# Layer norm behind the residual in the second and third attention layer: the row scaling goes from VectorE to ScalarE

## Chip, cores and metric

The kernel runs on one core of a Trainium2 chip. The metric is the time of one execution on the device, in microseconds (us), as the median of several runs. All the work here is float32 apart from a few small bf16 masks.

## The reference, cut to what matters

```
x = x + cross_attention_0(norm(x), ctx)            # layer 0
x = x + routed_attention_ffn(norm(x))              # the choice phase
h = norm(x)
h = _layernorm(h + self_attention(h), g1, b1)      # second layer of the attention code, "L1"
h = _layernorm(h + cross_attention(h, ctx), g2, b2)# third layer, "L2"
h = _layernorm(h + relu_ffn(h), g3, b3)            # late phase
x = x + h ;  x = x + moe_ffn(norm(x))              # late phase

def _layernorm(x, gamma, beta):
    mean = jnp.mean(x, axis=-1, keepdims=True)
    std = jnp.sqrt(jnp.mean((x - mean) ** 2, axis=-1, keepdims=True))
    return (x - mean) / (std + EPS) * gamma + beta
```

128 sequences of 64 tokens, width 128, 16 heads of depth 8. The change concerns `(x - mean) / (std + EPS)` of the layer norms with `g1, b1` and `g2, b2`. They stand behind the residual of L1 and L2.

## The kernel before

The 8192 tokens are cut into 16 groups of 512 tokens (8 sequences, 4 tiles of 128 rows). `attention_phase(..., (1, 2))` runs L1 and L2 as one pipeline of 32 steps. A step is one group's attention, and has eight slots `v` = 0 to 7, one for each unit of 8 heads on 128 tokens. In a step three groups are in work: the step's own group `g` (scores and softmax), the next group (its x, q, k and v are prepared: transposed, projected and copied, each in a slot of its own), and the group before (output projection, residual and layer norm, in two halves `m` = 0 and 1 of 256 tokens).

Each engine executes its own list in the order in which it is written, and the engines meet at semaphores. In slot `v`:

- TensorE (PE): in even slots the scores of units v and v+1 (L681, with a mask matmul at L668 or L675 ahead of it); the transposes of unit v-1 (L699), here T(v-1); the weighted sums of unit v-2 (L715), here W(v-2); then a preparation matmul if this slot has one (x transposes L642, q L648, k L646, v L651); in slots 0 and 4 the output's transpose (L724), in 1 and 5 the output projection (L733). T(7), W(6) and W(7) of a group run in slots 0 and 1 of the next step. Before each T(u) PE waits for VectorE's `shift(u)`.
- VectorE (DVE): `shift(v)` (the row maximum L491 and its subtraction L493), then the slot's other work: `divide`, `residual` of half 0 in slot 2 and of half 1 in slot 6, `normalise` of half 0 in slot 5 (L1) or 4 (L2), and `normalise` of half 1 at the end of slot 7, behind `shift(7)` and `divide`. The next instruction of DVE is then `shift(0)` of the next step.
- ScalarE (ACT): the exponential of unit v-1 (L398), then its preparation copies: in L1 the keys are spread in slots 5 and 6 (L365) and the values in slot 7 (L379); in L2 the keys in slots 0 and 1 and the values in slot 6.
- GpSimd (POOL): for each step the list is: inputs of the next group; `finish` of half 0; `with_bias` (L303, residual plus output bias, 128x512); `finish` of half 1. `finish` is a wait for the moments, the root `sd` (L309), a wait for `z_done`, then times gamma (L312) and plus beta (L315).

So the norm of one half goes DVE moments (L524), POOL root (L309), DVE `se`, `rs` and `z` (L531, L533, L536), POOL gamma and beta. In the last step of L2 there is no next group, so POOL's `with_bias` and all preparation are missing there.

Of the kernel before, what the change touches and what calls it, by code (L numbers as in the profile page):

```python
# [15 lines left out]
P = 128  # L16
# [96 lines left out]
def attention_phase(nc, ps, C, x_res, y_res, x_in, ctx_in, key_mask, run, ahead=(), setup=None):  # L113
# [11 lines left out]
    with ExitStack() as ctx:  # L125
        def sb(name, shape, dt=F32):
            return ctx.enter_context(nc.sbuf_tensor(f"{name}{a}", shape, dt))
# [34 lines left out]
        if post_norm:  # L162
            t1 = sb("t1", [P, 2, 2, D])
            st2 = sb("st2", [P, 2, 2, 6])
            mv2 = sb("mv2", [P, 2, 2, 2])
            sd2 = sb("sd2", [P, 2, 2])
            se2 = sb("se2", [P, 2, 2])
            rs2 = sb("rs2", [P, 2, 2])
            z2 = sb("z2", [P, 2, 2, D])
            zg2 = sb("zg2", [P, 2, 2, D])  # L170

# [38 lines left out]
        std2 = sem("std2")  # L210
        std2_eps = sem("std2_eps")
        rstd2 = sem("rstd2")
        z_done = sem("z_done")
        zg_done = sem("zg_done")
        y_done = sem("y_done")
# [60 lines left out]
        @block.gpsimd  # L276
        def _(pool):
            def rows_of(L, g):
                return tiles_of(x_res if L.a == 0 else y_res, L.own(g))

            def inputs_of(L, g, s, two_before):
                if L.pre_norm:
                    pool.wait_ge(var_eps, nth(g))
                    nc.gpsimd.tensor_tensor(rstd[:, :], veps[:, :], C["mhalf"][:, 0:TILES], ALU.pow
                                            ).then_inc(rstd_done, 1)
                    pool.wait_ge(rstd_done, nth(g))
                    nc.gpsimd.tensor_tensor(nmr[:, :], negmean[:, :], rstd[:, :], ALU.mult).then_inc(nmr_done, 1)
                else:
                    if two_before:

                        pool.wait_ge(prep_ready, nth(g - 2, NP, two_before.nr("xT")))
                        pool.sem_inc(passed, 1)
                    nc.gpsimd.tensor_copy(xn[:, s], rows_of(L, g)).then_inc(xn_ready, 1)

            def with_bias(L, g, s, first):
                if L.a == 1:
                    pool.wait_ge(xn_ready, nth(g))
                if not first:

                    pool.wait_ge(resid_done, g * 2 - 2)  # L300
                if L.a == 1 or not first:
                    pool.sem_inc(passed, 1)
                nc.gpsimd.tensor_tensor(xb[:, s], xn[:, s] if L.a == 1 else rows_of(L, g), across(L.bo, TILES), ALU.add  # L303
                                        ).then_inc(xb_ready, 1)

            def finish(L, g, m):
                if L.post_norm:
                    pool.wait_ge(moments2, nth(g, 2, m))
                    nc.gpsimd.tensor_tensor(sd2[:, m, :], mv2[:, m, :, 1], C["half"][:, 0:2], ALU.pow  # L309
                                            ).then_inc(std2, 1)  # L310
                    pool.wait_ge(z_done, nth(g, 2, m))
                    nc.gpsimd.tensor_tensor(zg2[:, m], z2[:, m], across(L.gam, 2), ALU.mult).then_inc(zg_done, 1)  # L312
                    pool.wait_ge(zg_done, nth(g, 2, m))
                    pool.sem_inc(passed, 1)
                    nc.gpsimd.tensor_tensor(tiles_of(y_res, L.own(g), 2 * m, 2), zg2[:, m], across(L.bet, 2), ALU.add  # L315
                                            ).then_inc(y_done, 1)

            def step(g, s, first, of, before, after):
                if after:
                    inputs_of(after, g + 1, 1 - s, before)  # L320
                if not first:

                    finish(before, g - 1, 0)
                if after:
                    with_bias(after, g + 1, 1 - s, first)
                if not first:

                    finish(before, g - 1, 1)
                if not after:
                    finish(of, g, 0)  # L330
                    finish(of, g, 1)

            def prep(g, s, L):
                if L.a == 0:
                    pool.wait_ge(consts_set, 1)
                    pool.wait_ge(pack_loaded, 16)
                inputs_of(L, g, s, None)
                with_bias(L, g, s, True)

            in_layers(pool, layers, prep, step)  # L340

        @block.scalar
        def _(act):
            def norm_apply(L, g, s, two_before):
                if not L.pre_norm:
                    return
                act.wait_ge(nmr_done, nth(g))
                if two_before:

                    act.wait_ge(prep_ready, nth(g - 2, NP, two_before.nr("xT")))  # L350
                    act.sem_inc(passed, 1)
                for t in range(TILES):
                    last = nc.scalar.activation(xn[:, s, t:t + 1, :], tiles_of(x_res, L.own(g), t, 1), ACT.Identity,
                                                bias=nmr[:, t:t + 1], scale=rstd[:, t:t + 1])
                last.then_inc(xn_ready, 1)
# [40 lines left out]
            def exps(g, u):  # L396
                act.wait_ge(t_ready, nth(g, UNITS, u))
                nc.scalar.activation(ex[:, u % 2], UB[u % 4].rearrange("p (c n) -> p c n", n=P), ACT.Exp  # L398
                                     ).then_inc(e_ready, 1)

            def copy_onT(L, g, m):

                act.wait_ge(onT_ready, nth(g, 2, m))
                nc.scalar.activation(onT[:, m], OB[m][:, 0:2 * P], ACT.Identity, bias=L.bv).then_inc(onT_copied, 1)
# [18 lines left out]
            def step(g, s, first, of, before, after):  # L423
                for v in range(UNITS):
                    if v > 0:
                        exps(g, v - 1)
                    elif not first:
                        exps(g - 1, UNITS - 1)
                    if v in (0, 4) and not first:
                        copy_onT(before, g - 1, v // 4)  # L430
                    if after:
                        prep_slot(after, g + 1, 1 - s, v)
                        if v == 2:
                            norm_apply(after, g + 1, 1 - s, before)
                if not after:
                    exps(g, UNITS - 1)
                    copy_onT(of, g, 0)
                    copy_onT(of, g, 1)

            act.wait_ge(vblk_set, 3)  # L440
            if a == 0:
                act.wait_ge(consts_set, 3)
            in_layers(act, layers, prep, step)

        @block.vector
        def _(dve):
# [60 lines left out]
            def residual(L, g, s, m):  # L507
                if m == 0:
                    dve.wait_ge(xb_ready, nth(g))
                dve.wait_ge(proj_ready, nth(g, 2, m))  # L510
                pr = PROJ[:, 256 * m:256 * m + 256].rearrange("p (t d) -> p t d", d=D)
                xs = xb[:, s, 2 * m:2 * m + 2, :]
                if not L.post_norm:
                    nc.vector.tensor_tensor(tiles_of(x_res, L.own(g), 2 * m, 2), pr, xs, ALU.add).then_inc(resid_done, 1)
                    return
                nc.vector.tensor_tensor(t1[:, m], pr, xs, ALU.add).then_inc(resid_done, 1)
                dve.wait_ge(resid_done, nth(g, 2, m))
                for t in (0, 1):
                    last = nc.vector.bn_stats(st2[:, m, t, :], t1[:, m, t, :])
                last.then_inc(stats2_done, 1)  # L520
                dve.wait_ge(stats2_done, nth(g, 2, m))
                dve.sem_inc(passed, 1)
                for t in (0, 1):
                    last = nc.vector.bn_aggr(mv2[:, m, t, :], st2[:, m, t, :])  # L524
                last.then_inc(moments2, 1)

            def normalise(L, g, m):
                if not L.post_norm:
                    return
                dve.wait_ge(std2, nth(g, 2, m))  # L530
                nc.vector.tensor_scalar(se2[:, m], sd2[:, m], EPS, None, ALU.add).then_inc(std2_eps, 1)  # L531
                dve.wait_ge(std2_eps, nth(g, 2, m))
                nc.vector.reciprocal(rs2[:, m], se2[:, m]).then_inc(rstd2, 1)  # L533
                dve.wait_ge(rstd2, nth(g, 2, m))
                for t in (0, 1):
                    last = nc.vector.tensor_scalar(z2[:, m, t, :], t1[:, m, t, :], mv2[:, m, t, 0:1],  # L536
                                                   rs2[:, m, t:t + 1], ALU.subtract, ALU.mult)
                last.then_inc(z_done, 1)

            def first_constants():  # L540
                nc.vector.memset(C["mhalf"][:, :], -0.5)
# [262 lines left out]
def nth(g, n=1, k=0):  # L804

    return g * n + (k + 1)
# [1418 lines left out]
```

## Time and profile before

| | us |
|---|---|
| median of 3 runs | 2162.67 (2158.76 to 2165.53) |
| the profiled execution | 2168.61 |
| its span in the trace | 2166.8 |
| L1 and L2 in the trace | about 642 to 1328 |
| one step of L1, in the middle | 21.6 |
| one step of L2, in the middle | 20.0 |

The times of the rows below are microseconds from the span's start. The profiled execution lies 6 us above the median of the runs. A step's length is the distance between the same instruction in two steps: `z` of half 1 starts at 822.91 and 844.53 in L1, and at 1275.38 and 1295.37 in L2.

### The profile page before, as it was taken

What the parts mean: (1) busy time and instruction counts of PE and PEld (TensorE: products, weight loads), DVE (VectorE), ACT (ScalarE), POOL (GpSimd) and SP (SyncE); (2) the same over time, 40 slices, a digit from 0 to 9 for tenths busy, and PEclk for the clock granted to TensorE, in tenths of its full rate; (3) what the DMA queues carried; (4) which work ended last, traced back from release to release, by engine and by line L of the source; (5) the groups of instructions that cost most, each with busy time, mean ns of one, the idle gap of its engine ahead of it and who ended that gap; (6) DMA issues with size and microseconds to landing.
All of it is one profiled execution on the core that took longest, in us unless ns stands there. A gap on an engine that the chain in (4) does not pass through costs nothing. (4 is left out here: it accounts for less than half of the span.)

```text
span 2166.8 us, 52756 instructions
## 1 busy us (share of the span) xinstructions
PE 1996.2 (92%) x19220; PEld 1546.9 (71%) x19220; DVE 1635.8 (75%) x4569; ACT 1065.2 (49%) x2180; POOL 465.8 (21%) x520
## 2 busy tenths in 40 slices
PE   7999994788869999999999998999999999999998
PEld 4666673666646666666666665767888888888887
DVE  5777776676536888888888884668888888888886
ACT  5656652556534555555545542543444444444442
POOL 1111110110101222222222222672211111112111
PEclk9999997999978999999999996999999999999999
DMA  3000000000000000000100002000000000000000
GB/s 126 30 29 27 21 10 1 1 1 0 1 20 2 0 0 0 0 0 21 30 29 19 29 10 66 1 1 1 11 6 5 6 10 5 6 5 10 5 5 10
DMA packets 27409, 30.50 MB, mean 14 GB/s; under 512 B 1952, under 2 KB 20640, under 8 KB 27040
## 3 DMA queue, kind: packets, MB, share of 16 engines
q1 hardware_dynamic: 27296, 29.18, 4.1%
q8 instruction: 48, 0.79, 0.1%
q14 instruction: 65, 0.53, 0.1%
HBM read 24.98 MB, written 4.19 MB: 13 GB/s over the span
## 5 line engine op out<-in xcount | busy, mean ns | idle before, releaser
L491 DVE TENSOR_REDUCE mx<-ps 128x8 f32<-128x512 f32 x384 | 262.3, 683 | 169.4 <-PE ps L681 169.3
L398 ACT ACTIVATE ex<-ps 128x512 f32<-128x512 f32 x384 | 230.2, 599 | 266.0 <-PE ps L699 263.8
L1125 ACT ACTIVATE y_res<-ps 128x512 f32<-128x512 f32 x288 | 172.4, 599 | 355.7 <-PE ps L1211 355.5
L1193 PEld LDWEIGHTS ps<-down,y_res 128*128 128x128 f32 x2048 | 267.2, 191 | 24.9 <-issue 3.0
L699 PE MATMUL ps<-pack,sh 128*128 128x128 f32 x1536 | 252.7, 287 | 27.6 <-DVE sh L493 26.8
L493 DVE TENSOR_TENSOR sh<-ps,mx 128x512 f32<-128x512 f32 x384 | 265.5, 691 | 13.2
L1193 PE MATMUL ps<-down,y_res 128*128 128x128 f32 x2048 | 270.5, 275 | 1.3 <-DVE y_res L1479 1.3
L715 PEld LDWEIGHTS ps<-vblk,ex 128*64 128x64 f32 x6144 | 214.7, 140 | 66.3 <-issue 66.3
L1461 DVE TENSOR_TENSOR y_res<-ps,y_res 128x512 f32<-128x512 f32 x288 | 197.9, 687 | 80.4 <-PE ps L1211 65.9
L715 PE MATMUL ps<-vblk,ex 128*64 128x32 f32 x6144 | 257.7, 227 | 0.0
L699 PEld LDWEIGHTS ps<-pack,sh 128*128 128x128 f32 x1536 | 170.3, 143 | 119.9 <-issue 63.7
L1479 DVE SCALAR_TENSOR_TENSOR y_res<-ps,late_comb,y_res 128x128 f32<-128x128 f32 x768 | 215.6, 344 | 23.8 <-PE ps L1193 11.6
L681 PE MATMUL ps<-kblk,qd 32*64 32x256 f32 x3072 | 208.3, 387 | 1.6 <-issue 1.5
L365 ACT ACTIVATE kblk<-ps,bkm,pack 128x512 f32<-128x512 f32 x192 | 139.0, 783 | 23.5 <-PE ps L646 23.5
L1209 PE MATMUL ps<-late_x_lo,late_gate_hi 128*128 128x512 f32 x288 | 136.7, 475 | 12.5 <-DVE y_res L1461 12.5
L681 PEld LDWEIGHTS ps<-kblk,qd 32*64 32x64 f32 x3072 | 108.8, 135 | 54.3 <-issue 9.9
L1031 POOL TENSOR_TENSOR y_res<-y_res 128x512 f32<-128x512 f32 x48 | 62.0, 1292 | 369.6 <-ACT y_res L1118 369.6
L1211 PE MATMUL ps<-late_x_hi,late_up_hi 128*128 128x512 f32 x288 | 114.2, 397 | 0.0
L1209 PE MATMUL ps<-late_x_lo,late_up_hi 128*128 128x512 f32 x288 | 113.6, 395 | 0.0
L1211 PE MATMUL ps<-late_x_hi,late_gate_hi 128*128 128x512 f32 x288 | 113.6, 394 | 0.0
L1210 PE MATMUL ps<-late_x_hi,late_gate_lo 128*128 128x512 f32 x288 | 112.5, 391 | 0.0
L1210 PE MATMUL ps<-late_x_hi,late_up_lo 128*128 128x512 f32 x288 | 111.8, 388 | 0.0
(237 smaller groups left out, 3419.8 us busy)
## 6 DMA issues: line engine op xcount, KB each, us to landing
ctxT<-in_ctx SPq DMA_DIRECT2D x32, 256.0 KB, 2.7
x_res<-in_x SPq DMA_DIRECT2D x16, 256.0 KB, 2.7
kmi<-in_key_mask SPq DMA_DIRECT2D x16, 256.0 KB, 3.2
out<-y_res SPq DMA_DIRECT2D x16, 256.0 KB, 2.3
pack<-in_pack SPq DMA_DIRECT2D x1, 2053.0 KB, 9.8
wqkv<-in_wqkv SPq DMA_DIRECT2D x1, 1536.0 KB, 10.9
gate<-in_gate SPq DMA_DIRECT2D x6, 192.0 KB, 3.7
up<-in_up SPq DMA_DIRECT2D x6, 192.0 KB, 3.7
```

The costliest lines, as they stand in the source:

```text
L398: nc.scalar.activation(ex[:, u % 2], UB[u % 4].rearrange("p (c n) -> p c n", n=P), ACT.Exp).then_inc(e_ready, 1)
L491: nc.vector.tensor_reduce(mx[:, u % 2], sc, AX.X, ALU.max).then_inc(max_done, 1)
L493: nc.vector.tensor_tensor(sh[:, u % 4].rearrange("p (h k) -> p h k", k=S), sc, mx[:, u % 2].unsqueeze(2).broadcast_to((P, HH, S)), ALU.sub ...
L681: last = nc.tensor.matmul(outs[w][64 * b:64 * b + 64, t * HQ * S:(t + 1) * HQ * S], qd[rows, s, n * S:(n + 1) * S], kblk[rows, s, n].rearr ...
L699: last = nc.tensor.transpose(UB[u % 4][:, c * P:(c + 1) * P], sh[:, u % 4, c * P:(c + 1) * P], ident)
L715: last = nc.tensor.matmul(OB[m][64 * b:64 * b + 64, col:col + 32], ex[:, u % 2, c, b * S:(b + 1) * S], vblk[:, s, 2 * (2 * m + t) + b, pai ...
L1193: last = nc.tensor.matmul(YB[k % 2][:, t * D:(t + 1) * D], act_[:, k % 3, t * P:(t + 1) * P], down[:, k, :], start=True, stop=True)
L1209: nc.tensor.matmul(out, hi, y, start=True, stop=False)
L1210: nc.tensor.matmul(out, lo, x, start=False, stop=False)
L1211: return nc.tensor.matmul(out, hi, x, start=False, stop=True)
L1461: V.tensor_tensor(act_[:, k % 3], UB[k % 2], sg[:, k % 2], ALU.mult).then_inc(act_ready, 1)
L1479: last = V.scalar_tensor_tensor(acc[:, s, t], y[:, t], comb[:, s, t, k - SH:k - SH + 1], acc[:, s, t], ALU.mult, ALU.add)
```

## The change

DVE no longer computes `z = (t - mean) * rs`. After `rs` it makes a bias for each row, `nm = -mean * rs` (128x2, one small instruction for both tiles of a half), and signals `nmr2_done`. ScalarE makes `z = t * rs + nm` with one ACTIVATE for each tile of 128 rows and signals `z_done`. It does so for half 0 at the end of its slot 6 and for half 1 at the end of its slot 7. `z_done` starts at 2, and DVE's `residual` waits until ScalarE has read the `t` of the group before, in the same buffer.

```
@@ pool: finish(L, g, m)
-                    pool.wait_ge(z_done, nth(g, 2, m))
+                    pool.wait_ge(z_done, nth(g, 2, m) + 2)
@@ scalar, new
+            def scale_rows(L, g, m):
+                if not L.post_norm:
+                    return
+                act.wait_ge(nmr2_done, nth(g, 2, m))
+                for t in (0, 1):
+                    last = nc.scalar.activation(z2[:, m, t:t + 1, :], t1[:, m, t:t + 1, :], ACT.Identity,
+                                                bias=nm2[:, m, t:t + 1], scale=rs2[:, m, t:t + 1])
+                last.then_inc(z_done, 1)
@@ scalar: step, at the end of slot v
+                    if v >= 6 and not first:
+                        scale_rows(before, g - 1, v - 6)
                 if not after:
...
+                    scale_rows(of, g, 0)
+                    scale_rows(of, g, 1)
@@ vector: residual
+                dve.wait_ge(z_done, nth(g, 2, m))
+                dve.sem_inc(passed, 1)
@@ vector: normalise
-                for t in (0, 1):
-                    last = nc.vector.tensor_scalar(z2[:, m, t, :], t1[:, m, t, :], mv2[:, m, t, 0:1],
-                                                   rs2[:, m, t:t + 1], ALU.subtract, ALU.mult)
-                last.then_inc(z_done, 1)
+                nc.vector.scalar_tensor_tensor(nm2[:, m], mv2[:, m, :, 0], -1.0, rs2[:, m], ALU.mult, ALU.mult
+                                               ).then_inc(nmr2_done, 1)
```

ScalarE's list at the end of a step of L2's loop, in the kernel before (`vblk` are the values of the next group, `ex` the exponentials of units 5, 6 and, in the next step, 7):

```order
L398 ACTIVATE ex<-ps 128x512
L376 REGISTER_ALU
L379 COPY vblk<-ps 64x4x8x8 x4
L397 REGISTER_ALU
L398 ACTIVATE ex<-ps 128x512
L397 REGISTER_ALU
L398 ACTIVATE ex<-ps 128x512
```

The same place in the changed kernel:

```order
L400 ACTIVATE ex<-ps 128x512
L378 REGISTER_ALU
L381 COPY vblk<-ps 64x4x8x8 x4
L408 ACTIVATE z<-t,nm,rs 128x128 x2
L399 REGISTER_ALU
L400 ACTIVATE ex<-ps 128x512
L408 ACTIVATE z<-t,nm,rs 128x128 x2
L399 REGISTER_ALU
L400 ACTIVATE ex<-ps 128x512
```

Half 0's `z` now stands behind the copy of the values, half 1's between the exponentials of units 6 and 7.

POOL's list for one step of L1's loop, which keeps its order, in the changed kernel:

```order
L310 ISA
L311 TENSOR_TENSOR sd<-mv,half 128x2
L313 REGISTER_ALU
L314 TENSOR_TENSOR zg<-z,pack 128x256
L317 ISA
L317 TENSOR_TENSOR y_res<-zg,pack 128x256
L302 ISA
L305 TENSOR_TENSOR xb<-xn,pack 128x512
L310 REGISTER_ALU
L311 TENSOR_TENSOR sd<-mv,half 128x2
```

The second `sd`, the root of half 1, stands behind half 0's gamma and beta and behind `xb`, before and after the change; what is new is the engine for whose `z` the first `zg` waits.

## Rows read from the trace of the kernel before

**Rows 1.** The page's slices of the span, 40 of 54.2 us each: granted TensorE clock in tenths.
```profile
PEclk9999997999978999999999996999999999999999
```

**Rows 2.** Windows: length, then busy us of PE, PEld, DVE, ACT, POOL; granted clock; DMA.
```profile
700.00:970.00 270.00, 258.23 (x3541) 176.95 (x3540) 222.84 (x607) 147.43 (x287) 78.96 (x111) 1.00 0.00 0
990.00:1298.00 308.00, 299.89 (x4124) 211.30 (x4118) 269.98 (x649) 157.75 (x293) 86.52 (x124) 1.00 0.08 24
1298.00:1328.00 30.00, 28.85 (x255) 20.41 (x254) 16.18 (x45) 6.20 (x11) 4.67 (x7) 0.51 0.00 1
642.00:664.00 22.00, 20.48 (x165) 12.07 (x164) 9.76 (x23) 6.49 (x14) 2.49 (x3) 0.51 0.00 1
```

**Rows 3.** Waits in L2, 990 to 1298 us: total, times, longest.
```profile
DVE mx L491 <- PE ps L681: 23.7, 31, 1.2
```

**Rows 4.** Groups by line, 640 to 1310 us: busy us, mean ns of one.
```profile
L536 DVE TENSOR_SCALAR z<-t,mv,rs 128x128 f32<-128x128 f32 x120 | 36.2, 344 | 2.2
L353 ACT ACTIVATE xn<-x_res,nmr,rstd 128x128 f32 (+1 forms) x60 | 24.6, 482 | 0.0
```

**Rows 5.** Timeline of L1, end of a step: start, duration, idle before.
```profile
840.60 1.44 ACT L365 ACTIVATE kblk<-ps,bkm,pack 128x512 f32<-128x512 f32 x2
...
841.45 1.28 POOL L303 TENSOR_TENSOR xb<-xn,pack 128x512 f32<-128x512 f32 x1 [1.47 <-DVE t L516]
...
842.69 0.71 POOL L309 TENSOR_TENSOR sd<-mv,half 128x2 f32<-128x2 f32 x1
...
844.14 0.16 DVE L531 TENSOR_SCALAR se<-sd 128x2 f32<-128x2 f32 x1
...
845.07 0.69 DVE L491 TENSOR_REDUCE mx<-ps 128x8 f32<-128x512 f32 x1
```

**Rows 6.** Timeline of L2, end of a step and start of the next.
```profile
1112.35 1.09 POOL L303 TENSOR_TENSOR xb<-y_res,pack 128x512 f32<-128x512 f32 x1 [3.14 <-DVE t L516]
...
1112.67 1.50 ACT L379 COPY vblk<-ps 64x256 f32<-64x256 f32 x4 [1.08 <-PE ps L651]
...
1113.40 0.71 POOL L309 TENSOR_TENSOR sd<-mv,half 128x2 f32<-128x2 f32 x1
...
1115.02 0.16 DVE L531 TENSOR_SCALAR se<-sd 128x2 f32<-128x2 f32 x1
...
1115.93 0.68 DVE L491 TENSOR_REDUCE mx<-ps 128x8 f32<-128x512 f32 x1
...
1116.10 0.64 POOL L312 TENSOR_TENSOR zg<-z,pack 128x256 f32<-128x256 f32 x1 [1.99 <-DVE z L536]
...
1117.02 0.64 POOL L315 TENSOR_TENSOR y_res<-zg,pack 128x256 f32 x1 [0.28 <-POOL zg L312]
...
1117.39 0.42 PEld L699 LDWEIGHTS ps<-pack,sh 128*128 128x128 f32 x4 [0.32 <-DVE sh L493]
```

**Rows 7.** Timeline of PE in L2: T(0), T(1) mid-loop, then in the last step.
```profile
1277.36 0.66 PE L699 MATMUL ps<-pack,sh 128*128 128x128 f32 x4
...
1280.38 0.66 PE L699 MATMUL ps<-pack,sh 128*128 128x128 f32 x4
...
1297.35 0.66 PE L699 MATMUL ps<-pack,sh 128*128 128x128 f32 x4 [0.99 <-DVE sh L493]
...
1301.86 1.11 PE L699 MATMUL ps<-pack,sh 128*128 128x128 f32 x4
```

**Rows 8.** A window of the choice phase: PE busy, then granted clock.
```profile
421.00:422.00 1.00, 0.00 (x0) 0.71 0.00 0
```

**Rows 9.** Timeline of PE in L1, T(1) and W(3): first step, then a later one.
```profile
650.34 1.11 PE L699 MATMUL ps<-pack,sh 128*128 128x128 f32 x4
...
663.08 0.95 PE L715 MATMUL ps<-vblk,ex 128*64 128x32 f32 x16
...
828.13 0.66 PE L699 MATMUL ps<-pack,sh 128*128 128x128 f32 x4
...
835.91 0.66 PE L715 MATMUL ps<-vblk,ex 128*64 128x32 f32 x16
```

More of the change, by code:

```diff
@@ L168, in attention_phase @@
             rs2 = sb("rs2", [P, 2, 2])
+            nm2 = sb("nm2", [P, 2, 2])
             z2 = sb("z2", [P, 2, 2, D])
@@ L212, in attention_phase @@
         rstd2 = sem("rstd2")
+        nmr2_done = sem("nmr2_done")
         z_done = sem("z_done")
@@ L442, in _ @@
                 act.wait_ge(consts_set, 3)
+            if post_norm:
+                act.sem_inc(z_done, 2)
             in_layers(act, layers, prep, step)
```

## The prediction

> **What bounds the kernel now.** I began with the slices of the span. L1 and L2 lie in slices 12 to 25, and the reader should see that the TensorE clock is granted in full there, but not in the slices at their two edges [rows 1]. The windows say the same in figures: in the middle of L1 PE is shown busy 258 us of 270, DVE 223 and ACT 147, in the middle of L2 300, 270 and 158 of 308 [rows 2]. DVE and PE bound these layers together. ACT is half idle, and to give it DVE's work looks free. The third view is the waits: DVE waits for scores about twice in a step (23.7 us in 31 waits over L2) [rows 3]. In those places a shorter DVE list buys nothing. The fourth is the timeline of a step's end, which decides here. PE stands before T(0) and waits 0.32 us for DVE's shift(0), which stands behind `normalise` of half 1 [rows 6]. So this `normalise` is on the path that sets the step's length, and whatever it waits for is too.
>
> **Half 0, taken from DVE.** `z` costs DVE 36.2 us over 60 halves, 0.60 us a half [rows 4]. For half 0 it stands in slot 5 (L1) or 4 (L2), and the next scores come late afterwards [rows 3]. I count nothing for its removal; the wait for scores grows by what is saved. `nm`, 128x2 on DVE, isn't in the trace. From below it costs 0 (then all 0.60 us are saved), from above 0.60, as much as the `z` that it replaces. The nearest row is `se`, also 128x2, with 0.16 us [rows 5]. I take 0.17, so a `normalise` gets 0.43 us shorter.
>
> **Half 0, put on ACT.** An ACTIVATE of 128x128 with scale and bias from a column is there already, 482 ns [rows 4], so two take 0.96 us. ACT has the time, but the place decides. In L1 the two stand behind the spread of the keys, which ends at 840.60 + 1.44 = 842.04 [rows 5]. In L2 they stand behind the copy of the values, which ends at 1112.67 + 1.50 = 1114.17 [rows 6]. Today half 0's `z` is long done by then. POOL waits for it, and behind POOL's wait stand, in this order, gamma, beta, `with_bias` and the root `sd` of half 1. DVE's `normalise` of half 1 waits for that root, and behind it stands shift(0). The chain is new:
>
> - L1: 842.04 + 0.96 (`z`) + 0.92 (start of gamma to start of beta [rows 6]) + 0.64 (beta [rows 6]) + 1.28 (`xb`) + 0.71 (`sd`) = 846.55. Today `se` starts at 844.14 [rows 5]. DVE comes 2.41 us later to it.
> - L2: 1114.17 + 0.96 + 0.92 + 0.64 + 1.09 + 0.71 = 1118.49, against 1115.02 [rows 6]: 3.47 us later.
>
> Hand-overs of about 0.1 us between engines are left out, and so is an overlap of the two ACTIVATEs; they roughly cancel. From each I take off the 0.43 us of the shorter `normalise`: shift(0), and T(0) behind it, come 2.0 us later in L1 and 3.0 in L2. All that PE can do ahead of T(0) it has then done, and nothing later in the step gives the time back, because each following pair of slots hangs on T(0) through scores and exponentials.
>
> How many steps: L1's loop has 14 (2.0 us each); the last step of L1, the first of L2 and L2's loop have L2's preparation slots, 16 steps (3.0 each). The last step of L2 has neither copy nor `with_bias`, so no stall, and the end of the layer costs under 1 us more. Sum: 28 + 48 = 76 us.
>
> **Half 1 on ACT.** It waits for `nm` and delays the exponential of unit 7. W(7), which needs that, stands behind T(0), and T(0) needs shift(0), 1.4 us of DVE work after `nm`; 0.96 us of `z` and the exponential fit within that and T(0) itself. Nothing, then; without that cover it would be up to 0.5 us a step. The exponential of unit 6 in L2 comes 0.96 us later, within the stall. The new wait of `residual` is for a `z` from the step before, done a slot or more earlier: nothing.
>
> **What the stall does to the clock.** PE's wait before T(0) grows from about 0.3 us to some 2.3 in L1 and 3.3 in L2. In the last step of L2 a wait of 0.99 us stands at the same place [rows 7], and from 1298 on the granted clock is at its lower level, 1.2 GHz, for the rest of that step (mean 0.51) [rows 2]. The only other difference there is that no key projection ran before the wait. In the choice phase the clock falls inside a stretch in which PE does nothing [rows 8]. I therefore expect a fall in each of the 30 stalled steps. How long does it stay down? In the first step of L1 it is down up to 664 (mean 0.51) and full later [rows 2]; 664 is just behind the q projection of slot 4, ahead of W(3) [rows 9]. So a visit lasts from T(0) to the q projection, if that suffices. Its price, from rows at both levels:
>
> - T(0) to T(1): 1301.86 - 1297.35 = 4.51 against 1280.38 - 1277.36 = 3.02 [rows 7], 1.5 us more.
> - T(1) to W(3), which follows q: 663.08 - 650.34 = 12.74 against 835.91 - 828.13 = 7.78 [rows 9], 5.0 us more.
>
> That is 6.5 us. A projection need not suffice: those of the prologue, ahead of 642, had not lifted the clock [rows 2]. Then it stays down to the next one, k in L1 a slot later or v in L2 two slots later, with the projection itself some 3 to 6 us of work (a slot is an eighth of a step, 2.5 to 2.7 us). At the ratio 12.74 / 7.78 = 1.64 that costs 2 to 4 us more. I give that 4 cases in 10 and take 8.0 us a visit (estimated from these rows). The price is bounded by 0 below (no fall) and 13 above (down for the whole step: 0.64 x 20.0 to 21.6). 30 x 8.0 = 240 us.
>
> **A rule of the skill.** The trace first: a wait of 0.99 us was enough for the fall [rows 7]. The Trainium skill, page "TensorE: Matmul & The Clock Gate", section "HAM oscillation", tells of a kernel whose clock falls in waits for a DMA of about 3 to 5 us, longer than L1's stall. By that the clock would fall in L2 at most: the second rival. The trace doesn't agree with it as a lower bound, at least where little matmul work surrounds the wait.
>
> **The sum.** 2168.6 + 76 + 240 = 2484.6 for the profiled execution. It lay 6 us above the median of the runs, so I predict 2479 us.
>
> **Rivals.**
>
> 1. *The clock holds.* Only the stall: 2163 + 76 = 2239 us. For it: mid-loop, L1 and L2 hold the full clock over short waits [rows 2]. Against: [rows 7], with a third of the stall.
> 2. *The clock falls in L2 alone*, where the stall is longest: 76 + 16 x 8 = 204, 2367 us. L1's stall is 2.0 us with the value projection and the mask matmuls close ahead, which speaks a little for it.
> 3. *The clock stays down through nearly all of both layers.* PE is then last itself and hides the stall: 30 x 13 = 390, 2553 us. For it: 22 us at a stretch at the start of L1 [rows 2]. Against: the loops bring three projections a step.
> 4. *Faster.* If POOL had half 1's root ready before DVE reached `se`, only the 0.43 us would count, and T(0) can move by 0.32 at most, since PE then bounds it: 30 x 0.3 = 9 us, 2154. It decides at ACT: half 0's `z` would have to end about 3.4 us before 1115.02, at 1111.6 in L2, ahead of the copy of the values, which starts only at 1112.67 [rows 6]. The list of ACT excludes that, unless the hardware did the POOL work much faster than its rows.
> 5. *Nothing measurable:* the late `z` takes some other slack that I don't see. Nothing in the profile speaks for it.
>
> **Chances.** Forecast 0.60, rival 1 0.12, rival 2 0.13, rival 3 0.08, rival 4 0.03, rival 5 0.04. A measurement of this kernel tells 0.3% (6.5 us) from no change. That gives slower 0.93, within 0.3% 0.04, faster 0.03. The likeliest case alone has 2430 to 2530 (6.5 to 9.5 us a visit). The range goes down to rival 1 and up just short of rival 3: 2235 to 2540.
>
> **What would show it.** In the changed profile: DVE's `se` of half 1 idle 2.4 us (L1) and 3.4 us (L2) with POOL's root as the one that ended the wait; POOL's gamma of half 0 released by ACT's `z`, at the end of ACT's keys or values; PE's T(0) waiting for `sh` for 2 to 3 us; steps of about 31 to 32 us where they were 21.6 and 20.0; granted clock around 0.7 to 0.8 in the slices of both layers, rising behind a projection; all other phases as long as before. I am wrong on the stall if `se` waits under 1 us; on the clock if the slices of both layers read 1.00; on the direction if T(0) doesn't wait longer than 0.3 us.

## Result and profile after

The changed kernel takes 2444.92 us (median of 6 runs, 2443.73 to 2448.55) against 2164.1 us before (6 runs): 1.1304 times as long, 95% interval 1.1279 to 1.1329, or 280.8 us more. It is slower, as forecast; the predicted time of 2479 us was 34 us too high. The executions of the kernel before differ among themselves: of the 23 measured beside the first four experiments, 12 have a mean granted clock of 0.970 or more and a median of 2160.8 us, 11 have 0.965 to 0.968 and 2168.9 us; the profiled one (0.967) is of the second kind.

The page after, the same rows of slices as [rows 1], now 61.1 us each. L1 and L2 lie in slices 11 to 27:

```profile
DVE  5777766765365555556555555547788888888886
ACT  5666625666344444444333333345444434444343
POOL 1111111110022222221111111137411111111211
PEclk9999979999687777778777777779999999999999
```

Every engine, ACT too, is now less busy there, and from slice 13 to 27 the granted clock reads 7 (once 8) instead of 9. The windows, as in [rows 2] (length, busy us of PE, PEld, DVE, ACT, POOL, clock). The middle of L1, then the middle of L2:

```profile
700.00:970.00 270.00, 248.78 (x2491) 164.52 (x2487) 149.94 (x406) 118.01 (x238) 53.07 (x76) 0.72 0.00 0
1150.00:1560.00 410.00, 368.22 (x3617) 246.98 (x3616) 234.04 (x543) 159.52 (x309) 73.61 (x107) 0.72 0.05 16
```

DVE was busy for 223 of the same 270 us of L1 before and is busy for 150 now: it gets through two thirds of the work in the same time. Outside the two layers nothing changed: in the choice phase (335 to 640 us) PE is busy 219.6 us before and 219.4 after. Layer 0 and the late phase, first before, then after:

```profile
0.00:335.00 335.00, 307.30 (x4036) 217.23 (x4036) 231.98 (x530) 196.04 (x385) 39.87 (x52) 1.00 0.12 39
1340.00:2166.00 826.00, 802.05 (x4921) 690.65 (x4919) 654.69 (x2096) 360.20 (x727) 202.68 (x171) 1.00 0.03 9
```

```profile
0.00:335.00 335.00, 307.77 (x4036) 217.66 (x4036) 231.80 (x530) 195.81 (x385) 39.88 (x52) 1.00 0.12 39
1617.00:2442.00 825.00, 800.89 (x4921) 689.13 (x4919) 654.16 (x2096) 359.86 (x727) 202.67 (x171) 1.00 0.03 9
```

The same late work that began at 1340 begins at 1617; the loss is between. The waits from 700 to 1500 us (total, times, longest) name it:

```profile
POOL zg L314 <- ACT z L408: 463.9, 52, 17.3
...
DVE mx L508 <- PE ps L699: 201.3, 79, 3.4
...
DVE se L551 <- POOL sd L311: 71.2, 26, 3.4
PE ps L717 <- DVE sh L510: 71.0, 40, 3.2
```

The third row didn't exist before: DVE waits for POOL's root in each of the 26 steps, 2.7 us on average. The second was 1.2 us at most in L2 [rows 3] and is the larger one now: DVE waits for scores, because PE is slow. The end of a step of L1, answering to [rows 5] (start, duration, idle before):

```profile
904.03 0.88 ACT L408 ACTIVATE z<-t,nm,rs 128x128 f32<-128x128 f32 x2
...
904.99 0.64 POOL L314 TENSOR_TENSOR zg<-z,pack 128x256 f32<-128x256 f32 x1 [15.88 <-ACT z L408]
...
905.90 0.64 POOL L317 TENSOR_TENSOR y_res<-zg,pack 128x256 f32 x1 [0.28 <-POOL zg L314]
906.49 1.27 POOL L305 TENSOR_TENSOR xb<-xn,pack 128x512 f32<-128x512 f32 x1
...
907.72 0.71 POOL L311 TENSOR_TENSOR sd<-mv,half 128x2 f32<-128x2 f32 x1
...
908.46 0.17 DVE L551 TENSOR_SCALAR se<-sd 128x2 f32<-128x2 f32 x1 [2.14 <-POOL sd L311]
...
909.41 0.69 DVE L508 TENSOR_REDUCE mx<-ps 128x8 f32<-128x512 f32 x1 [0.39 <-issue]
...
910.88 1.11 PE L717 MATMUL ps<-pack,sh 128*128 128x128 f32 x4 [2.48 <-DVE sh L510]
```

This is the predicted chain, link by link: ACT's `z`, gamma, beta, `xb`, root, `se`, shift(0), T(0). T(0)'s four transposes took 0.66 us before [rows 7] and take 1.11 here. The windows around it (PE's busy time, then the clock):

```profile
909.00:910.00 1.00, 0.00 (x0) 1.00 0.00 0
910.00:911.00 1.00, 0.12 (x1) 0.93 0.00 0
911.00:928.00 17.00, 17.00 (x138) 0.50 0.00 0
```

PE stands still, and as T(0) starts the clock falls. It stays at 1.2 GHz for 20.5 us here, which is the longest of the 28 falls between 690 and 1560; 24 of them last 17.1 us, three 13.7. The fall comes from 0.1 us before to 2.0 us after the start of T(0), so behind the wait rather than in it. From one fall to the next a step is then 30.7 us long in L1 and in L2 alike (once 34.1 us, three times 27.3), where it was 21.6 and 20.0.

### The profile page after: what moved, and what is told of

The parts are those of the page before. It is cut to its first block and busy times, and to the rows that moved or that the text cites. A ratio compares the mean times of both kernels' runs of the same rounds, so it can differ in the third digit from the quotient of the medians.

```text
span 2442.5 us, 52940 instructions
## 1 busy us (share of the span) xinstructions
PE 2205.7 (90%) x19220; PEld 1667.8 (68%) x19220; DVE 1617.7 (66%) x4505; ACT 1114.7 (46%) x2308; POOL 464.4 (19%) x520
## 5 line engine op out<-in xcount | busy, mean ns | idle before, releaser
L717 PE MATMUL ps<-pack,sh 128*128 128x128 f32 x1536 | 301.6, 329 | 90.8 <-DVE sh L510 90.8
L717 PEld LDWEIGHTS ps<-pack,sh 128*128 128x128 f32 x1536 | 203.5, 165 | 204.0 <-DVE sh L510 109.5
L733 PEld LDWEIGHTS ps<-vblk,ex 128*64 128x64 f32 x6144 | 257.0, 164 | 87.8 <-issue 80.6
L733 PE MATMUL ps<-vblk,ex 128*64 128x32 f32 x6144 | 302.4, 248 | 3.1 <-ACT ex L400 3.0
L699 PE MATMUL ps<-kblk,qd 32*64 32x256 f32 x3072 | 258.4, 463 | 1.5 <-issue 1.5
L699 PEld LDWEIGHTS ps<-kblk,qd 32*64 32x64 f32 x3072 | 128.9, 162 | 78.1 <-issue 48.7
L314 POOL TENSOR_TENSOR zg<-z,pack 128x256 f32<-128x256 f32 x64 | 40.7, 636 | 549.4 <-ACT z L408 549.4
```

Source lines behind the costliest of these rows:

```text
L699: last = nc.tensor.matmul(outs[w][64 * b:64 * b + 64, t * HQ * S:(t + 1) * HQ * S], qd[rows, s, n * S:(n + 1) * S], kblk[rows, s, n].rearr ...
L717: last = nc.tensor.transpose(UB[u % 4][:, c * P:(c + 1) * P], sh[:, u % 4, c * P:(c + 1) * P], ident)
L733: last = nc.tensor.matmul(OB[m][64 * b:64 * b + 64, col:col + 32], ex[:, u % 2, c, b * S:(b + 1) * S], vblk[:, s, 2 * (2 * m + t) + b, pai ...
```

## Experiments

All ratios are against runs of the kernel before on the same chip.

**Half 0 scaled a slot earlier.**

```
-                    if v >= 6 and not first:
-                        scale_rows(before, g - 1, v - 6)
+                    if v in (5, 7) and not first:
+                        scale_rows(before, g - 1, v // 7)
```

> The changed kernel, but ScalarE scales half 0 at the end of slot 5 instead of slot 6; half 1 stays at the end of slot 7. Theory A (the place of half 0's z on ScalarE makes GpSimd late with half 1's root): half 0's z ends at about 840.0 in L1 and 1109.5 in L2 (on the time scale of the kernel before), GpSimd is back at its old times, VectorE's se waits for nothing, the clock stays full: 2150 to 2168 us. Rival B (the two-way trip of half 1, nm to ScalarE and back, or ScalarE's added work, costs the time): it stays above 2400 us.

Measured: 2156.89 us against 2163.71, ratio 0.9959 (0.9937 to 0.998). One slot of ACT's list is worth 288 us. The middle of both layers:

```profile
700.00:970.00 270.00, 259.29 (x3562) 177.69 (x3554) 213.83 (x584) 167.41 (x338) 77.22 (x110) 1.00 0.00 0
990.00:1290.00 300.00, 293.47 (x4067) 208.25 (x4060) 255.86 (x603) 176.28 (x346) 84.92 (x122) 1.00 0.08 25
```

ACT does all the added work here, and the clock is full. So neither this work nor half 1's trip to ACT is the cause.

**GpSimd's roots first.** ScalarE stays as changed.

```
                 if not first:
-                    finish(before, g - 1, 0)
+                    root(before, g - 1, 0)
                 if after:
                     with_bias(after, g + 1, 1 - s, first)
                 if not first:
-                    finish(before, g - 1, 1)
+                    root(before, g - 1, 1)
+                    affine(before, g - 1, 0)
+                    affine(before, g - 1, 1)
```

(`root` is the wait for the moments and `sd`, `affine` the rest of `finish`.)

> The changed kernel with ScalarE as it is, but GpSimd's list in another order: root of half 0, with_bias, root of half 1, and only then gamma and beta of both halves. Theory A (the queue on GpSimd carries the delay): half 1's root no longer stands behind the wait for half 0's z, so no stall and a full clock: 2150 to 2170 us. Rival C (ScalarE's own order, z ahead of the exponentials of units 6 and 7, delays PE): a part of the 280 us stays, time above 2250.

Measured: 2163.35 us, ratio 0.9984 (0.9959 to 1.0009), no difference. POOL's timeline in L1:

```profile
885.96 1.28 POOL L305 TENSOR_TENSOR xb<-xn,pack 128x512 f32<-128x512 f32 x1 [9.77 <-DVE t L540]
887.19 0.71 POOL L311 TENSOR_TENSOR sd<-mv,half 128x2 f32<-128x2 f32 x1
887.87 0.64 POOL L317 TENSOR_TENSOR zg<-z,pack 128x256 f32<-128x256 f32 x1
```

The root of half 1 now comes before half 0's gamma. ACT's late `z` does no harm once nothing urgent is queued behind POOL's wait for it. With the run before, this closes the chain from both ends: it needs the late `z` and POOL's order.

**The changed kernel with PE kept busy.** In slot 0, ahead of T(0), matmuls whose result isn't used:

```
+                    if post_norm and not first and after and v == 0:
+                        for _ in range(3 if after.a == 1 else 5):
+                            nc.tensor.matmul(PROJ[:, 0:2 * P], ident, pk[:, 0:2 * P], start=True, stop=True)
```

> The changed kernel, with 3 (step prepares an L1 group) or 5 (L2 group) added float32 matmuls of 128x128 by 256 columns on PE ahead of T(0), written to columns of the projection bank that are overwritten later; the stall of VectorE stays. Theory A with the clock as its larger term: PE has work during the wait, the granted clock stays full, and only the stall of 76 us remains: 2225 to 2260 us. Rival D (the stall alone costs 280 us and the low clock is only a sign of it): the time stays near 2445 or rises.

Measured: 2252.65 us, ratio 1.0395 (1.0341 to 1.0449), 89 us over before and 192 us under the changed kernel, though PE has more to do. The two windows of L1 and L2, and from the waits between 700 and 1290 us the stall, still there:

```profile
700.00:1000.00 300.00, 278.90 (x3692) 193.18 (x3685) 218.45 (x594) 169.33 (x342) 77.77 (x112) 1.00 0.00 0
1030.00:1360.00 330.00, 310.25 (x3964) 220.83 (x3964) 243.37 (x570) 169.49 (x330) 78.74 (x114) 1.00 0.07 21
```

```profile
DVE se L551 <- POOL sd L311: 67.7, 25, 3.4
```

DVE waits 2.7 us a step as in the changed kernel, but the clock is full. This separates the two terms: the stall costs 89 us at most, the clock 192. The traces give the stall more closely. From T(0) of the first stalled step to T(0) of the last (29 steps) it is 602.4 us before, 679.8 here and 877.8 in the changed kernel, so 77 us for the stall of 29 steps, about 80 for all 30, and 198 us for the clock. The rest of the 89 lies outside these steps. The added matmuls also shorten PE's own wait ahead of T(0), to 0.7 to 1.2 us in L1 and at most 1.0 in L2.

**Only half 0 on ScalarE.** `scale_rows` for half 0 alone, in slot 6; half 1's `z` as before.

```
-                    if v >= 6 and not first:
-                        scale_rows(before, g - 1, v - 6)
+                    if v == 6 and not first:
+                        scale_rows(before, g - 1, 0)
```

> Only half 0 is scaled by ScalarE (end of slot 6); half 1's z stays on VectorE. Theory A: the stall is there in full, without the shorter normalise: se waits 2.4 (L1) and 3.5 us (L2), the clock falls in each step, 2430 to 2480 us. Rival B (half 1's trip is the cause): about 2165 us.

Measured: 2463.79 us, ratio 1.1366 (1.1312 to 1.1419). The whole loss is there, 19 us more than with both halves; the clock falls 28 times before the last step of L2.

**Only half 1 on ScalarE.**

```
-                    if v >= 6 and not first:
-                        scale_rows(before, g - 1, v - 6)
+                    if v == 7 and not first:
+                        scale_rows(before, g - 1, 1)
```

> Only half 1 is scaled by ScalarE (end of slot 7); half 0's z stays on VectorE. Theory A: GpSimd has half 0's z in time, no stall, full clock; half 1's normalise is shorter by up to 0.43 us, T(0) earlier by at most 0.32: 2152 to 2168 us. Rival B (half 1's trip or the wait for nm costs something of its own): above 2172.

Measured: 2158.73 us, ratio 0.9967 (0.9945 to 0.999). Half 1's move is a small gain: 4.6 us of the 602.4 us between T(0) of the first and of the last of the 30 steps, by the traces.

**A delay and nothing else.** The kernel before, with n = 1, 2 and 4 reductions into a tile that nobody reads, between half 1's `normalise` and shift(0):

```
                             normalise(before, g - 1, 1)
+                            if before.post_norm and after:
+                                for i in range(n):
+                                    nc.vector.tensor_reduce(dead[:, i], C["ff1"].rearrange("p (h k) -> p h k", k=S),
+                                                            AX.X, ALU.max)
```

> The kernel before, with one added reduction of 128x512 (0.69 us) on VectorE between half 1's normalise and shift(0), in every step in which the change has its stall; nothing else is changed. T(0) waits 0.3 + 0.7 = 1.0 us. If the clock holds, the cost is the delay alone, 30 x 0.7 = 21 us: 2185. If this wait is enough for the clock, as 0.99 us was in L2's last step, 2300 to 2420. I hold the first for likelier in most steps, since here a projection stands close to the wait.

> As the run with one added reduction, but two (1.38 us): T(0) waits 1.7 us. Delay alone: 30 x 1.4 = 41 us, 2205. If the clock falls in all steps: near 2445, since the change and this then spend the same stretch of each step at half clock. I expect the second in most steps, 2350 to 2445.

> As before, with four added reductions (2.76 us) and no ScalarE or GpSimd work moved: T(0) waits 3.1 us, about the change's stall in L2, more than in L1. If the change's cost is the stall and the clock and nothing else, 2430 to 2490; if something else of the change costs (ScalarE's order, GpSimd's late gamma and beta), clearly less than 2430.

| added reductions | median us | ratio (interval) | over before | falls of the clock, 690 us to the last step of L2 |
|---|---|---|---|---|
| 1 | 2187.1 | 1.0104 (1.0069 to 1.0139) | 25 | 0 |
| 2 | 2283.36 | 1.0535 (1.0468 to 1.0602) | 121 | 10 in L1, 1 in L2 |
| 4 | 2430.04 | 1.1212 (1.1144 to 1.1279) | 268 | 13 in L1, 12 in L2 |

The medians are of 7, 2 and 2 executions. The last step of L2, where the clock falls in the kernel before too, is left out of the last column; it falls there in all three.

With one, the delay alone is paid for, and T(0) waits 0.81 us in L1:

```profile
875.91 0.66 PE L704 MATMUL ps<-pack,sh 128*128 128x128 f32 x4 [0.81 <-DVE sh L494]
```

With two, T(0) waits 1.40 us in L1. In this step its transposes already run at the lower clock, which lasts for 17 us:

```profile
835.31 0.97 PE L704 MATMUL ps<-pack,sh 128*128 128x128 f32 x4 [1.40 <-DVE sh L494]
```

```profile
834.00:835.00 1.00, 0.00 (x0) 1.00 0.00 0
835.00:836.00 1.00, 0.69 (x4) 0.76 0.00 0
836.00:852.00 16.00, 16.00 (x136) 0.50 0.00 0
```

The second reduction of 0.64 us costs 96 us, the first 25. With four, and nothing of ScalarE or GpSimd moved, 268 of the change's 281 us are lost, with waits of 2.59 us in L1 and 2.1 to 2.5 in L2: a late shift(0) is enough for the loss.

My expectation for two was too high: the clock held in nearly all steps of L2, where a key projection runs just ahead of T(0). The projection also shortens PE's wait there, to 0.9 to 1.3 us. But the length of the wait alone doesn't decide: 0.99 us let the clock fall in the last step of L2 of the kernel before [rows 7], where all preparation is missing, and with two reductions it held in L2 over the same wait:

```profile
1236.54 0.66 PE L704 MATMUL ps<-pack,sh 128*128 128x128 f32 x4 [0.99 <-DVE sh L494]
```

Nor does a projection alone protect: with four reductions the clock fell in 12 of the 15 steps of L2 that have one. The projection ahead shows in the changed kernel too: the step that prepares the first group of L2 but still computes L1's scores is the only one between 700 and 1100 us without a fall, and its wait is 1.22 us instead of 2.0 to 2.5. Its PE timeline (L664 is the key projection):

```profile
1094.52 1.13 PE L664 MATMUL ps<-ctxT,pack 128*128 128x512 f32 x2
...
1095.48 0.38 PE L742 MATMUL ps<-pack,on 128*128 128x128 f32 x2
...
1097.08 0.66 PE L717 MATMUL ps<-pack,sh 128*128 128x128 f32 x4 [1.22 <-DVE sh L510]
```

**Two reductions, with PE work ahead of T(0) in L1.** As with n = 2, and:

```
+                    if post_norm and not first and after and after.a == 1 and v == 0:
+                        for _ in (0, 1):
+                            nc.tensor.matmul(PROJ[:, 0:2 * P], ident, pk[:, 0:2 * P], start=True, stop=True)
```

> The kernel before with two added reductions (1.4 us) on VectorE ahead of shift(0), as in the run with the two alone, and two added matmuls of 128x128 by 256 columns on PE ahead of T(0) in L1's steps. The run with two reductions alone lost its clock in 11 steps of L1 and in one of L2, where a key projection runs just ahead of T(0). If PE's work close to the wait decides, the clock now holds in L1 as well, and only the delay is left: 30 x 1.4 = 41 us, 2200 to 2212. If the length of VectorE's delay decides, it stays near 2283.

Measured: 2213.23 us, ratio 1.0236 (1.019 to 1.0281). One microsecond of matmuls a step takes 70 us off the 2283, with DVE's delay in place, to 1 us above the range expected. The middle of L1 with two reductions alone, and with the matmuls:

```profile
700.00:970.00 270.00, 253.52 (x2697) 0.76 0.00 0
```

```profile
700.00:970.00 270.00, 254.64 (x3399) 1.00 0.00 0
```

DVE's delay by itself doesn't cost the clock; it depends on what PE does beside it. The matmuls do two things, though: they fill PE ahead of T(0), and they shorten its wait from 1.40 to 0.54 us, less than the 0.81 us that cost nothing. Which of the two holds the clock, this run doesn't show. In L2, where nothing was added, the clock fell in one step here as well (at 1186 us).

**The last step of L2.** There the clock falls in the kernel before too [rows 7]. Added to before, and to the kernel with half 0 a slot earlier:

```
+                    if post_norm and not after:
+                        if v == 0:
+                            for _ in (0, 1):
+                                nc.tensor.matmul(PROJ[:, 0:2 * P], ident, pk[:, 0:2 * P], start=True, stop=True)
+                        if v in (3, 4, 6):
+                            nc.tensor.matmul(PREP, ident, pk[:, 0:512], start=True, stop=True)
```

> The kernel before, with added float32 matmuls in the last step of L2 alone (two of 256 columns ahead of T(0), one of 512 columns in slots 3, 4 and 6), where the clock fell at 1298 after a wait of 0.99 us. If PE's missing work let it fall, it now holds there: the last step gets some 8 us shorter net of the 4 us that the matmuls take, 2150 to 2160 us. If not, 2164 to 2170.

> The run with half 0 scaled at the end of slot 5, with the same matmuls added in the last step of L2. If the two gains add: 2143 to 2153 us, below the 2157 of the one alone and the 2163 of before; if the clock doesn't hold in the last step, 2157 to 2162.

Measured: 2161.34 us, ratio 0.9982 (0.9957 to 1.0008), and 2156.86 us, ratio 0.997 (0.9946 to 0.9994). Neither can be told from the same kernel without the matmuls, where I had expected some 8 us. In the first, T(0) of the last step no longer waits at all, and the fall moved from 1298 to 1322 us. All its 12 executions have a mean granted clock of 0.974 to 0.976; of the 23 of the kernel before measured beside them 12 have less than 0.970 (median 2170.3 us) and 11 have 0.972 to 0.975 (2159.1 us). It may be that the matmuls only take away the slower of these and cost in the others what they give; this stays open. The lowest medians are those with half 0 a slot earlier, 2156.89 alone and 2156.86 with the matmuls, which thus gain nothing there.

## Why the prediction was right, and what it had too large

**What bounds the kernel: right.** The path ran through half 1's `normalise`, and ACT's free time was no measure of what a place in its list costs.

**The chain: right**, in order and size. `z` ended 0.96 us after its start in my sum and 0.88 in the trace (both tiles together), and the hand-overs took the rest. DVE's wait for the root came out at 2.14 us in L1 and 3.35 in L2 against 2.41 and 3.47. One reading was loose: the 0.32 us of [rows 6] is a wait of the weight load. PE's transposes waited 0.22 to 0.30 us in L1 and not at all in L2's loop.

**The shorter `normalise`: half of it at most.** I took 0.43 us off each stall. `nm` takes 160 ns, as estimated, but in every second step shift(0) still starts 0.95 us after `se`, with 0.39 us of "issue" between, about as late as with the long `z` (0.93 us in [rows 5]); in the others it starts 0.51 us after. On average that saves 0.2 us instead of 0.43. In L1 the error cancels against the shorter wait for the root, which is luck: with PE kept busy a step of L1 takes 23.66 us, 2.0 more than the 21.65 before, as forecast. In L2 it takes 23.2, 3.2 more instead of 3.0. So the stall cost about 80 us against 76. Why DVE loses this time in every second step, I did not test; the loop body has two steps, so its end is near at hand.

**Half 0's z gone from DVE is worth nothing: right.** Only half 1 on ACT gains 3 us, both (a slot earlier) 7, and the two intervals overlap. By the traces both gain the same: 597.8 and 597.9 us from T(0) of the first to T(0) of the last of the 30 steps, against 602.4. So half 1 adds no loss of its own, and the new wait of `residual` none either.

**The clock falls in the stalled steps: right.** It fell in 29 of the 30. The exception is the last step of L1, with the key projection ahead that I had named as the difference to the last step of L2, and with a shorter wait of PE. One of the 29 is the last step of L2, to which the thirtieth stall delays shift(0), and there it fell before the change too. So 28 falls are new, where I had charged 30.

**The price of a visit: too large.** This is most of the 34 us. I took 6.5 us for a visit that ends behind the q projection, and 1.5 for 4 in 10 that miss it. None missed it: in the changed kernel all 28 end 1.5 to 4.8 us after the q projection starts, three of them just as the k projection has begun. 192 to 198 us over 28 are 6.9 to 7.1 us a visit, close to the 6.5 from rows at both levels [rows 7, 9]. Those 6.5 are themselves a little low, because the two stretches of [rows 9] don't hold the same work: the first step of L1 has no output transpose behind q, the later step has (0.38 us at full clock). Of the profiled executions, 2484.6 us was forecast and 2444.3 measured, 40 less. The clock's term (8.0 x 30 = 240 against 198) is 42 too large, the stall's 4 too small.

**The rivals.** The clock holds: 2239, no; but the run with PE kept busy is that kernel, at 2253. The clock falls in L2 alone: no, and the other way round. With two reductions it fell in 10 steps of L1 and one of L2. I had read the work ahead of the wait wrongly: the value projection of L1 is followed by the scores, T(7) and W(6) before PE stands still, the key projection of L2 by the output's transpose alone. Whether that order or L2's shorter wait made the difference, no run separates. The clock down throughout: no, since it rises behind q in each step. Faster: excluded by ACT's order, as written; the kernel with half 0 a slot earlier is what that rival would have needed, and at 2157 us it comes close to the 2154.

**The rule of the skill.** In the two-reduction run waits of 1.40 us ahead of T(0) let the clock fall in 10 of the 13 steps of L1 that have this wait, and in the last step of L2 of the kernel before 0.99 us did [rows 7]. The Trainium skill, page "TensorE: Matmul & The Clock Gate", section "HAM oscillation", describes falls in DMA waits of about 3 to 5 us. This case's traces don't bear out that shorter waits are safe, and the measurement decides.

## What to carry to other kernels

Before moving work to an idle engine, find the place where its result is waited for, and read what is queued behind that wait, on the waiting engine and on those behind it: the idle share says nothing about lateness. Where TensorE works in small, sparse matmuls, a stall of 2 to 3 us a step can cost more through the clock than by its length (here 192 us beside some 80 to 89); put a dense matmul, useful if there is one, into the gap, ahead of the instruction that waits. A cause of two terms is best separated by removing one and keeping the other, as the matmuls ahead of T(0) did here.

## What the runs showed that I had not expected

- The loss isn't smooth in the delay: 0.81 us of wait in L1 costs no clock, 1.40 us costs it in 10 of 13 steps.
- With the clock falling and rising once a step, steps of L1 and L2 become equally long (30.7 us), though they differ by 1.6 us before the change and by 0.4 us with the stall at full clock.
- One short DVE instruction in place of two longer ones need not let the next one start earlier (0.39 us of "issue" ahead of shift(0) in every second step).
- GpSimd's `pow` takes 0.71 us for two numbers a row, more than its multiplication of 256 (0.64 us).
